# Normalised x split as it lies and turned by one DMA transpose, wider spare products, V's bias four steps sooner

## The reference

```
xn = layernorm(x);  q = xn Wq + bq;  k, v = ctx Wk + bk, ctx Wv + bv
x  = x + tanh(g0) * (softmax(q k' / 4) v Wo + bo)
h  = qdq(layernorm(x));  up = qdq(h Wup);  gate = qdq(h Wgate)
gate = qdq(gate * q16(sigmoid(gate)));  o = qdq(gate * up)
y  = x + tanh(g1) * (o Wdown)
```

## Time and profile before

| | |
|---|---|
| median of 3 runs | 587.12 us |
| profiled execution | 587.7 us |
| its span, first to last instruction | 585.9 us |
| TensorE busy | 545.1 us, 93% |
| VectorE busy | 482.0 us, 82% |
| ScalarE busy | 435.1 us, 74% |
| GpSimd busy | 191.9 us, 33% |
| mean granted clock of TensorE | 0.98 |

### The profile page before, as it was taken

How to read it: one execution, slowest core, us unless ns; L and a number is a source line. 1 busy time by engine, 2 the same in 40 slices (tenths; PEclk the granted TensorE clock), 3 DMA queues, 4 the chain that set the end, 5 groups by cost and what they waited for, 6 DMA issues and landing times. The chain is left out here.

```text
span 585.9 us, 12203 instructions
## 1 busy us (share of the span) xinstructions
PE 545.1 (93%) x4566; PEld 316.3 (54%) x4566; DVE 482.0 (82%) x818; ACT 435.1 (74%) x633; POOL 191.9 (33%) x298
## 2 busy tenths in 40 slices
PE   6779999999999998999787999999999899989998
PEld 2435555655565555555354444444444344468887
DVE  5587889999999999988657899979878799955432
ACT  2317898888788887887763454479999998889860
POOL 3411347776777788753562000000000000010000
PEclk9968999999999999999997999999999999989999
DMA  7322445445534554333220211000000000013443
GB/s 230 103 91 76 136 125 154 141 145 153 165 115 154 152 151 128 118 106 107 80 83 38 48 25 37 0 1 0 2 0 1 0 1 1 0 73 109 146 143 109
DMA packets 47808, 50.47 MB, mean 86 GB/s; under 512 B 15638, under 2 KB 35526, under 8 KB 47750
## 3 DMA queue, kind: packets, MB, share of 16 engines
q1 hardware_dynamic: 45766, 44.71, 25.0%
q0 software_dynamic: 1408, 4.46, 2.5%
q10 hardware_dynamic: 576, 0.52, 0.3%
HBM read 24.25 MB, written 8.63 MB: 56 GB/s over the span
## 5 line engine op out<-in xcount | busy, mean ns | idle before, releaser
L924 DVE TENSOR_REDUCE negm<-s_ps 128x2 bf16<-128x512 f32 x256 | 163.6, 684 | 15.1 <-PE s_ps L529 14.4
L732 ACT ACTIVATE pt<-st_ps 128x512 f32<-128x512 f32 x256 | 138.2, 594 | 40.5 <-PE st_ps L546 39.8
L1281 PE MATMUL pairs<-xq,wut 128*128 128x512 f16 x576 | 124.7, 379 | 2.7 <-ACT lnall L1472 1.6
L1281 PEld LDWEIGHTS pairs<-xq,wut 128*128 128x128 f16 x576 | 56.2, 98 | 71.1 <-issue 2.3
L529 PE MATMUL s_ps<-kst,qst 63*128 63x256 f16 x512 | 66.8, 281 | 17.6 <-DVE negm L924 13.5
L456 PE MATMUL pv_ps<-pt,vt 128*32 128x256 f32 x1024 | 68.5, 385 | 1.5 <-ACT ot L659 0.7
L1795 POOL PARTITION_ALL_REDUCE vmax<-vmax x5 | 1.8, 355 | 190.4 <-DVE vmax L1585 119.3
L1281 PE MATMUL pairs<-xq,wgt 128*128 128x512 f16 x276 | 59.7, 379 | 0.0
L546 PE MATMUL st_ps<-qst,kst 64*128 64x256 f16 x512 | 56.4, 272 | 1.7 <-ACT pt L732 1.7
L529 PEld LDWEIGHTS s_ps<-kst,qst 63*128 63x128 f16 x512 | 20.6, 94 | 55.5 <-DVE negm L924 39.7
L1383 PE MATMUL pairs<-wdt,h 128*128 128x256 f16 x384 | 48.3, 277 | 2.3 <-DVE h L1750 2.3
(11 more groups left out here) (231 smaller groups left out, 1035.3 us busy)
## 6 DMA issues: line engine op xcount, KB each, us to landing
qst<-qk SPq DMA_DIRECT2D x47, 128.0 KB, 2.1
kst<-qk SPq DMA_DIRECT2D x45, 128.0 KB, 2.1
xt<-in_x SPq DMA_DIRECT2D x16, 256.0 KB, 4.4
ct<-in_ctx SPq DMA_DIRECT2D x16, 256.0 KB, 3.0
xr<-in_x SPq DMA_DIRECT2D x16, 256.0 KB, 4.0
out<-y SPq DMA_DIRECT2D x16, 256.0 KB, 3.8
lnall<-out POOLq DMA_DIRECT2D x8, 512.0 KB, 4.3
recb<-rec_dram SPq DMA_DIRECT2D x15, 256.0 KB
```

The source lines that it names most:

```text
L732: nc.scalar.activation(pt[:, (j // 2) % 2, j % 2, :, r], st_ps[u % 3][:], ACT.Exp, scale=1.0 / (WS * WS * HD ** 0.5)).then_inc(exp_done, 1)
L924: nc.vector.tensor_reduce(negm[:, b % 2, :, lo], s_ps[r][:], AX.X, ALU.max, negate=True).then_inc(max_done, 1)
L1281: mm = nc.tensor.matmul(ps[:, p, k, :], w[:, a, dt, f * P:(f + 1) * P], xq[:, b, c, dt, :], start=n == 0, stop=n == len(terms) - 1)
```

## The change

1. x is split as it lies. ScalarE casts `xn` from SBUF to `xtok[:, 0]` at offset XH = -24 (residue 0), GpSimd subtracts to `xtok[:, 1]` at XL = -23 (residue 1), and the sync queue turns both halves by one DMA transpose into `xtr` at XDMA = -20 (residue 4), the diff's "step 4 of a batch". Batch 0 keeps the way over TensorE, but into `st_ps[1]`. The projection of q reads `xtr`.
2. `misc` has six users now; they alternate between its two banks.
3. `spare_products` reads `idle`, 128 rows of `pt` that VectorE zeroes first of all, and writes `st_ps[2]`. Two of them are added in each of steps -7 to -2.
4. V's bias product and its three VectorE operations move to step -10.
5. Products that nobody reads are added between and behind the last weight turns (1 each, 5 at the end) and ahead of the down products (11 instead of 4).
6. Two semaphores that guarded small operations in the feed-forward go.

```
     TURN, Q, K, V, TOP0, TOP1, PROJ = -18, -15, -13, -11, -4, 0, 23
+    XH, XL, XDMA = -24, -23, -20
-        xh = sb("xh", [P, 2, S], F16)
-        xl = sb("xl", [P, 2, S], F16)
+        xtok = sb("xtok", [P, 2, KT * D], F16)
+        xtr = sb("xtr", [P, 2, KT, 2, P], F16)
+        idle = pt[:, 0, 0, 0, 0, :].bitcast(F16)
...
-            return misc[(7 * (g // PAIRS) + (0, 1, 1, 2, 3, 4, 5, 6)[g % PAIRS]) % 2]
+            return misc[{TOP1 % PAIRS: 0, Q % PAIRS: 1, K % PAIRS: 0, TOP0 % PAIRS: 1, V % PAIRS: 0, PROJ % PAIRS: 1}[g % PAIRS]]
...
         @block.sync
+                if (b := batch(g, XDMA)) is not None and b:
+                    sp.wait_ge(xl_done, b + 1)
+                    sp.wait_ge(xh_done, b + 1)
+                    sp.wait_ge(q_done, b)
+                    sp.dma_start_transpose(xtr[:].rearrange("p i t u q -> p (i t u) q"),
+                                           xtok[:].rearrange("p i c -> p (i c)")).then_inc(x_turned, 16)
...
         @block.tensor
             def spare_products(n):
                 for _ in range(n):
-                    nc.tensor.matmul(s_ps[0][:].rearrange("p a b -> p (a b)"), kst[0:63, 1, 0, 0:P],
-                                     kst[0:63, 1, 0:2].rearrange("p j q -> p (j q)"), start=True, stop=True)
+                    nc.tensor.matmul(st_ps[2][:].rearrange("p a b -> p (a b)"), idle[:, 0:P], idle, start=True, stop=True)
+            def idle_products(n):
+                for _ in range(n):
+                    nc.tensor.matmul(s_ps[0][:].rearrange("p a b -> p (a b)"), wo2[:, 0, 0, 0:P],
+                                     wo2[:, 0].rearrange("p a b -> p (a b)"), start=True, stop=True)
...
                 if (b := batch(g, Q)) is not None:
                     pe.wait_ge(y_done, before(g, PROJ))
-                    pe.wait_ge(v_taken, before(g, V))
+                    pe.wait_ge(top_done[0], before(g, TOP0))
...
                     pe.wait_ge(xl_done, b + 1)
-                    project(bank(g), "q", xh, xl, q_done)
+                    if b:
+                        pe.wait_ge(x_turned, 16 * b)
+                    project(bank(g), "q", lambda k: xtr[:, 0, :, k, :], lambda k: xtr[:, 1, :, k, :], q_done)
...
-                if g == -6:
+                if -8 < g < -1:
+                    spare_products(2)
+                if g == -10:
                     pe.wait_ge(bv_spread, 1)
...
-                if (b := batch(g, TURN)) is not None:
-                    pe.wait_ge(top_done[0], before(g, TOP0))
-                    pe.wait_ge(ql_done, before(g, Q))
-                    pe.wait_ge(xl_done, b)
-                    pe.wait_ge(xn_ready, b + 1)
-                    to = bank(g)
+                if g == TURN:
+                    pe.wait_ge(xn_ready, 1)
...
                     for n in range(3, 8):
                         turn_weights(n // 4, n % 4)
+                        if n > 3:
+                            idle_products(1 if n < 7 else 5)
...
         @block.scalar
+                if (b := batch(g, XH)) is not None and b:
+                    act.wait_ge(xn_ready, b + 1)
+                    act.wait_ge(x_turned, 16 * (b - 1))
+                    nc.scalar.copy(xtok[:, 0], xn[:].rearrange("p t d -> p (t d)")).then_inc(xh_done, 1)
...
         @block.vector
+            nc.vector.memset(idle.bitcast(I32), 0).then_inc(kst_zeroed, 1)
...
-                if (b := batch(g, -17)) is not None:
-                    dve.wait_ge(xh_done, b + 1)
-                    nc.vector.tensor_tensor(xl[:], bank(PAIRS * b + TURN)[:], xh[:], ALU.subtract).then_inc(xl_done, 1)
+                if g == TURN + 1:
...
-                if g == -5:
+                if g == -10:
                     dve.wait_ge(gate_done, 1)
...
+                if g == -6:
                     dve.wait_ge(wo_high, 1)
...
         @block.gpsimd
-                    pool.wait_ge(xt_done, b)
+                    if b == 1:
+                        pool.wait_ge(xt_done, 1)
+                    else:
+                        pool.wait_ge(xh_done, b)
+                        pool.wait_ge(xl_done, b)
...
+                if (b := batch(g, XL)) is not None and b:
+                    pool.wait_ge(xh_done, b + 1)
+                    pool.wait_ge(x_turned, 16 * (b - 1))
+                    nc.gpsimd.tensor_tensor(xtok[:, 1], xn[:].rearrange("p t d -> p (t d)"), xtok[:, 0], ALU.subtract
+                                            ).then_inc(xl_done, 1)
...
 feed_forward
-            spare_products(ps[:, 0, 1], 4)
+            spare_products(ps[:, 0, 1], 11)
```

More of the change, by code:

```diff
@@ L619, in _ @@
                 if (b := batch(g, TOP1)) is not None:
-                    pe.wait_ge(xl_done, before(g, TURN))
-                    pe.wait_ge(top_done[0], before(g, TOP0))
+                    pe.wait_ge(v_taken, before(g, V))
+                    pe.wait_ge(kl_done, before(g, K))
                     pe.wait_ge(max_done, UNITS * b + UNITS)
@@ L643, in _ @@
             nc.tensor.matmul(pv_ps[:, 1, 0:1], row1[:], ltop[:], start=True, stop=True).then_inc(lmax_moved, 1)
-            for _ in range(2):
-                nc.tensor.matmul(s_ps[0][:].rearrange("p a b -> p (a b)"), wo2[:, 0, 0, 0:P],
-                                 wo2[:, 0].rearrange("p a b -> p (a b)"), start=True, stop=True)
+            idle_products(2)
         @block.scalar
@@ L713, in _ @@
                     high(1, bank(PAIRS * b + K), kh_done)
-                if (b := batch(g, -17)) is not None:
[L715 to L724, removed]
+                if g == TURN + 1:
+                    act.wait_ge(xt_done, 1)
+                    nc.scalar.copy(xtr[:, 0].rearrange("p t u q -> p u t q"),
+                                   st_ps[1][:].rearrange("p u (t q) -> p u t q", t=KT)).then_inc(xh_done, 1)
+                    act.wait_ge(kst_zeroed, 2)
+                    act.wait_ge(kl_done, 1)
+                    for d, i in enumerate((2, 3, 2)):
+                        act.dma_start(kst[d:P:4, 0].rearrange("p j q -> p (j q)"),
+                                      qk[:, i].rearrange("p h q -> p (h q)")).then_inc(stack_loaded[0], 16)
+                    weight_high("v", wv_loaded)
                 if 0 <= it < NB:
@@ L972, in _ @@
                     ln_max(LAST)
-                if (b := batch(g, -17)) is not None:
-                    dve.wait_ge(xh_done, b + 1)
-                    nc.vector.tensor_tensor(xl[:], bank(PAIRS * b + TURN)[:], xh[:], ALU.subtract).then_inc(xl_done, 1)
+                if g == TURN + 1:
+                    dve.wait_ge(xh_done, 1)
+                    nc.vector.tensor_tensor(xtr[:, 1].rearrange("p t u q -> p u t q"),
+                                            st_ps[1][:].rearrange("p u (t q) -> p u t q", t=KT),
+                                            xtr[:, 0].rearrange("p t u q -> p u t q"), ALU.subtract).then_inc(xl_done, 1)
                 if g == -16:
@@ L1795, in over_partitions @@
                 nc.gpsimd.partition_all_reduce(vmax[:, i, 1:2], vmax[:, i, 0:1], P, RMAX).then_inc(all_max, 1)
-            nc.gpsimd.partition_all_reduce(warm[:], t["lmaxall"][:], P, RMAX).then_inc(warmed, 1)
+            nc.gpsimd.partition_all_reduce(warm[:], t["lmaxall"][:], P, RMAX)
             for n, i in enumerate((0, 4, 1, 2, 3)):
```

35 lines of the change are left out of this document (17 added, 18 removed).

## The result

The changed kernel takes 582.03 us (median of 5 runs, 581.61 to 582.96); the kernel before, on the same chip, 588.12 us (585.24 to 588.25). The ratio is 0.992, with a 95% interval from 0.989 to 0.994. It is faster, by 6.1 us between the medians, where I forecast 9.5. The time lies inside the range that was to hold 8 in 10 (572.5 to 584 us), 0.5 us above the likeliest band (574 to 581.5). The profiled spans are 585.9 and 580.0 us, so the two traces hold nearly the whole difference between the medians.

A forecast was written before the change was run, and what follows sets the result against it. Bounds: VectorE's work per batch, the start before it saturates, and half-clock stretches of TensorE. Terms 1.6 + 1.8 + 0.4 + 4.1 + 0.6 + 1.0 = 9.5 us gained, from 587.1 to 577.6 us; 572.5 to 584 holds 8 in 10.

The forecast's parts named there:

- likeliest band: Whole kernel: time between 574 and 581.5 us, around the forecast of 577.6, given chance 0.60.
- The steady batches: Attention batches: x's turns and split leave TensorE and VectorE; mean 0.37 us in each of 11 batches, 4.1 us.
- The floor: Residue 6's last maxima to the next batch's first maximum: TensorE's order at residue 7 allows no less than 2.43 us.
- The two batches before these: Batches at 60 and 76 us, without output projection: 0.2 us gained each, 0.4 us together.
- The start: Up to step 0: first maximum 1.3 us sooner, then 17.8 us instead of 18.1 to step 0; 1.6 us gained.
- the wait for xn: Start: ScalarE's cast of batch 1's x waits for xn ahead of q's halves, limiting the first maximum's gain to 1.3 us.
- Steps 0 to 2: First two steps from step 0: full instead of half clock gains 1.8 us if spare products hold it, otherwise 0.
- The tail and the down product: Behind attention: idle products gain 0.6 us at the first gate products, spare products 1.0 us at the down products.
- GpSimd's subtraction, the cast on ScalarE, the DMA transpose: New operations per batch: covered by waits and idle time, cost taken as 0; the subtraction bounded by 0 and 0.5.
- rival 3: Sync queue: DMA transpose ahead of k's stack makes it late; at 1 us per batch 14 us, 591.6 us; chance 0.08.
- Rival 2: Clock not held: spare products don't raise it, prelude stays cold; gain only 1.6 us, 585.5 us; chance 0.10.

The follow-up runs named there:

- long_proj: Changed kernel with hold_zero's edit and two more 256-column products heading each output projection at residue 7; 582.27 us, ratio 0.994 against the kernel before.
- start_held: Changed kernel with the edits of q_first and hold_zero, and TensorE's idle stretches around the first scores filled with spare products; 576.07 us, ratio 0.983 against the kernel before.
- q_first: Changed kernel with ScalarE's cast of batch 1's x moved behind q's halves of batch 0; 579.54 us, ratio 0.991 against the kernel before.
- hold_zero: Changed kernel with two more 128-row spare products in each of steps -1 and 0; 579.56 us, ratio 0.990 against the kernel before.
- x_only: Kernel before with only the change's x path and bank order; old spare products, V's bias at step -6 and old ends; 587.16 us, ratio 1.001.
- no_spares: Changed kernel without its two spare products in each of steps -7 to -2; 581.80 us, ratio 0.994 against the kernel before.
- old_tail: Changed kernel without idle products behind the last weight turns and with 4 instead of 11 ahead of the down product; 583.77 us, ratio 0.998 against the kernel before.

## Why the prediction was right in sign and wrong in size

By its own steps:

- **The steady batches**, forecast 4.1, gained 2.7 over the same eleven. The mechanism was right: VectorE's relief is cut by TensorE's order at residue 7 (long_proj). Two sizes were off. The floor was 2.43 us by my sum and 2.54 by the rows, because only the first score product may start ahead of the last maximum; the others follow it, and TensorE's stretch is 2.19 us (106.17 to 108.36), not 1.96. And I took the mean of the distances as if all could fall to the floor: three batches were at it already, and three have extra work on VectorE beside residue 6 and are bound by it above the floor. So this mechanism brought 2.1 us. The other 0.5 is chance: one pair of clips beside GpSimd's work took 2.78 us before (at 219.07) and 2.26 after (at 217.55). The two batches before these gained 0.5 us each at their ends, not 0.2, but the clips took 0.6 back (last section).
- **The start**: the first maximum came at 23.86 (forecast 23.7), by the wait for xn that I had named. The way to step 0 was forecast 17.8 and took 18.7. I had taken Q's product of batch 1 cold, "as for one cold stretch up to step -6"; the stretch went on through step -6, whose two spare products took 0.5 us each (1.04 us from 29.82), up to 31.0. So the fillers of step -6 stood in VectorE's way instead of lifting the clock, and taken together the twelve brought next to nothing on this way (18.8 us without them). start_held shows the way out: with TensorE kept busy around the first scores, Q's product takes 1.3 us from 24.15 instead of 2.5, and from the first maximum to step 0 it is 18.1 us instead of q_first's 21.6.
- **Steps 0 to 2**, the step that failed: "1.8 us gained, if the two spare products in each of steps -7 to -2 hold the clock". They do not; 0.5 us came. The stretch that decides is steps -1 and 0, which have none, and in which VectorE's maxima leave TensorE idle. hold_zero put four products there and got the 3.7 us; start_held, which has them too, did not in its profiled execution (4.9). So none of these kernels reached 3.7 without them, and they are not always enough.
- **Not foreseen**, a term that my sum did not have: the clock fell at 75.4 us as well, which costs 1.35 us against hold_zero. I had treated TensorE's lighter load only as a relief. Removing the transposes of x from residue 6 takes work from TensorE in the only batches that have no output projection yet, and the fall occurs only with the new way of x; but it is not strict: x_only, no_spares and the changed kernel have it, the nine other kernels with the new way don't, in one profiled execution of each. So the lighter load as its cause is argued and not shown, and what decides it stays open.
- **The tail and the down product**, forecast 0.6 and 1.0: 2.1 and 1.2. The idle products are worth 2.1 us against old_tail and 1.7 against the kernel before, for the half clock had also held up the chain from the last maximum to the first gate products and those behind, which I had left out. 0.7 us of the tail is chance (last section). Behind the first down product 0.9 us came, but old_tail is as fast there (66.51 us) without the seven products on which the forecast rested.
- **GpSimd's subtraction, the cast on ScalarE, the DMA transpose**, forecast 0. The transposes landed in 3.1 to 6.2 us and TensorE never waited for them in a steady batch, so rival 3 is out. ScalarE's cast waited once, 2.1 us for a landing (up to 25.3 us); neither VectorE nor TensorE waited for ScalarE there. GpSimd cost something in a place that I had not looked at (below).

Rival 2, the clock not held, was the nearer miss: its early half came true in part and its late half did not. The errors partly cancel: by the table 5.3 us too much up to the last batches, and 1.7 too little behind them. That the time lies in the range owes something to this luck.

## What to carry to other kernels

Cheap filler products work where TensorE would idle and the engine that bounds the step waits for TensorE next; look for the sparse stretch right ahead of the expensive product, and don't put them where the work is dense anyway. When work is taken off TensorE, allow for one more clock fall as well as the relief: three of twelve kernels with the new way of x had one in the profile. When a relief per batch is a distance minus a floor, take each batch's own distance and its own second floor, not the mean; and a new wait is a free place, into which other work of that engine can go.

## What the runs showed of the hardware

**A VectorE copy from SBUF to SBUF ends behind GpSimd's instruction.** The copy of reciprocals at the end of the attention, 128x512 f32, took 0.43 us where GpSimd was all but done (a first copy, at 299.50 before). Where GpSimd's sum (128x512 f32, two SBUF inputs) ran, it ended 0.27 to 0.29 us behind it: before, GpSimd until 304.68 and the copy from 303.70 to 304.95; after, until 301.39 and 301.11 to 301.68; in hold_zero until 299.02 and 298.14 to 299.31. VectorE's timeline, before and after:

```profile
303.70 1.25 DVE L854 COPY wi<-recl 128x512 f32<-128x512 f32 x1
```

```profile
301.11 0.57 DVE L874 COPY wi<-recl 128x512 f32<-128x512 f32 x1
```

So 0.7 us of the change's gain is a matter of phase. The same in the early batches. The new order lets GpSimd normalise x without waiting for the transposes, hence sooner, and the sum that follows in its order now falls beside VectorE's clip. GpSimd's timeline, then VectorE's, of the changed kernel:

```profile
69.06 1.09 POOL L1073 TENSOR_SCALAR xn<-xt,rstd,shift 128x256 f32<-128x256 f32 x2 [0.30 <-POOL shift L1058]
70.12 1.05 POOL L1155 TENSOR_TENSOR wstage<-wstage,bi 128x512 f32<-128x512 f32 x1
```

```profile
70.40 1.38 DVE L1037 TENSOR_SCALAR wstage<-wi 128x512 f32<-128x512 int16 x2
```

The first of the two clips ends at 71.45, again 0.28 us behind GpSimd's sum (71.16). Before, GpSimd waited 4.19 us for the transposes, and both clips took 0.75 us: 0.6 us lost. VectorE's timeline, then GpSimd's, of the kernel before:

```profile
72.02 0.75 DVE L1013 TENSOR_SCALAR wstage<-wi 128x512 f32<-128x512 int16 x2
```

```profile
74.56 1.09 POOL L1045 TENSOR_SCALAR xn<-xt,rstd,shift 128x256 f32<-128x256 f32 x2 [4.19 <-PE misc L612]
```

GPSIMD Engine Reference of the Trainium skill, Key points, states that the two engines share SBUF interfaces and contend when VectorE is in a 2-port mode or has two SBUF inputs; these rows agree that the two get in each other's way. The copy and the clip have one SBUF input each, and whether they ran in a 2-port mode no trace here shows. I had used the rule only for the new subtraction, not for the old instructions that the change moves.

**The clock fell without a long pause of TensorE.** Ahead of the fall at 44.6 us TensorE had waited 0.89, 0.24, 0.27 and 0.32 us, for VectorE's maxima, in the 3 us before; with the fillers of hold_zero it waited 0.36 and 0.24 us in the same steps, and the clock stayed at 2.4 GHz. In start_held, with the same fillers and waits of 0.35 and 0.24 us there, it fell at 39.5 us, so these waits alone don't decide. TensorE's timeline of the changed kernel:

```profile
41.72 0.27 PE L546 MATMUL s_ps<-kst,qst 63*128 63x256 f16 x1 [0.89 <-DVE negm L945]
42.23 0.39 PE L546 MATMUL s_ps<-kst,qst 63*128 63x256 f16 x3 [0.24 <-DVE negm L945]
...
43.31 0.28 PE L546 MATMUL s_ps<-kst,qst 63*128 63x256 f16 x1 [0.27 <-DVE negm L945]
43.91 0.39 PE L546 MATMUL s_ps<-kst,qst 63*128 63x256 f16 x3 [0.32 <-DVE negm L945]
```
